# Delta-rule recurrence: the turned tile of updates, stored by value index instead of by lane, and read by the matmuls with a stride

## What is computed

```python
def step(S, inp):
    qt, kt, vt, at, bt = inp
    err = jnp.einsum('bhij,bhj->bhi', S, kt) - vt
    S = at[..., None] * S - bt[..., None, None] * (err[..., None] * kt[:, :, None, :])
    o = jnp.einsum('bhij,bhj->bhi', S, qt)
    return (S, o)
_, o = lax.scan(step, S0, xs)
```

## Time and profile before

| | |
|---|---|
| median of 3 runs | 3909.24 us (3908.29 to 3912.09) |
| span of the profiled execution | 3907.8 us |
| stretch with the recurrence | about 160 to 2345 us, 64 chunks of some 34 us |
| busy, whole span | PE 82%, DVE 76%, PEld 61%, POOL 56%, ACT 52% |

### The profile page before, as it was taken

The page is one execution under the profiler, slowest core; times in us unless marked ns, Lnnn a source line. Parts: engine busy times, 40 slices in busy tenths (PEclk is TensorE's granted clock), DMA queues, the critical chain, the costliest instruction groups (busy, mean ns, idle before and its releaser), DMA issues. The chain is left out here.

```text
span 3907.8 us, 126216 instructions
## 1 busy us (share of the span) xinstructions
PE 3194.9 (82%) x53441; PEld 2377.5 (61%) x53441; DVE 2965.5 (76%) x6600; ACT 2040.0 (52%) x4394; POOL 2182.6 (56%) x2735
## 2 busy tenths in 40 slices
PE   3678888887888888788888854759999899898989
PEld 2556666665666666666666644636666567656765
DVE  4488888888888888888888882058888788847884
ACT  2334444444444444444444423338887699728982
POOL 1367776767767677776767663431101188508860
PEclk7889999999999999999999975879999999999999
DMA  2111111111101111110111104100000012101111
GB/s 74 31 40 41 29 50 33 44 40 39 43 29 49 34 42 41 36 47 27 45 32 40 37 27 135 44 22 2 2 2 2 20 29 45 32 19 28 40 37 27
DMA packets 155957, 140.03 MB, mean 36 GB/s; under 512 B 64976, under 2 KB 108236, under 8 KB 155138
## 3 DMA queue, kind: packets, MB, share of 16 engines
q1 hardware_dynamic: 153090, 129.25, 12.0%
q0 software_dynamic: 2304, 2.71, 0.2%
HBM read 96.12 MB, written 16.82 MB: 29 GB/s over the span
## 5 line engine op out<-in xcount | busy, mean ns | idle before, releaser
L1235 DVE TENSOR_TENSOR a_tmp<-a_h,banks 128x128 f32<-128x128 f32 (+6 forms) x896 | 436.0, 487 | 29.9 <-DVE a_h L1212 0.2
L1241 DVE TENSOR_REDUCE a_h<-a_tmp 128x64 f32<-128x128 f32 (+6 forms) x896 | 432.2, 482 | 8.8
L940 POOL TENSOR_TENSOR a_st<-a_st,a_ab 128x512 f32<-128x512 f32 x256 | 322.1, 1280 | 0.0
L694 PE MATMUL banks<-a_wt,a_kt 32*64 32x64 f32 x8192 | 163.1, 258 | 145.8 <-DVE a_wt L1278 141.1
L552 PE MATMUL banks<-a_xseg,a_w_q 128*128 128x128 f32 x2048 | 247.0, 277 | 38.9 <-ACT a_kq L766 36.1
L2105 ACT ACTIVATE c_s<-c_s,c_low 128x384 f32<-128x384 f32 (+1 forms) x512 | 266.3, 579 | 19.1 <-DVE c_low L2049 13.7
L694 PEld LDWEIGHTS banks<-a_wt,a_kt 32*64 32x64 f32 x8192 | 153.6, 166 | 198.2 <-DVE a_wt L1278 169.8
L552 PEld LDWEIGHTS banks<-a_xseg,a_w_q 128*128 128x128 f32 x2048 | 234.3, 191 | 48.3 <-ACT a_kq L766 41.7
L2049 DVE CUSTOM_DVE_ANT_0 c_s<-banks,c_band 128x384 f32<-128x384 f32 (+1 forms) x512 | 245.5, 517 | 23.6 <-PE banks L1974 23.6
L552 PE MATMUL banks<-a_xseg,a_w_k 128*128 128x128 f32 x2048 | 241.5, 277 | 21.4 <-DMA a_xseg<-xn 18.4
L2150 POOL TENSOR_TENSOR c_qm<-c_qT,c_heads 128x512 f32<-128x512 f32 x32 | 33.3, 1040 | 396.3 <-PE banks L1974 395.9
(11 more groups left out here) (318 smaller groups left out, 8888.8 us busy)
## 6 DMA issues: line engine op xcount, KB each, us to landing
a_ab<-decays SPq DMA_DIRECT2D x512, 128.0 KB, 3.0
d_Vs<-d_V SPq DMA_DIRECT2D x128, 128.0 KB, 2.3
sent<-k_nothing SPq DMA_DIRECT2D x40, 64.5 KB, 2.3
b_xe<-sent SPq DMA_DIRECT2D x8, 322.5 KB, 3.4
a_xseg<-xn SPq DMA_DIRECT2D x32, 70.0 KB, 2.5
a_xrow<-in_L_attn_x SPq DMA_DIRECT2D x128, 16.0 KB, 1.8
x<-a_xrow SPq DMA_DIRECT2D x128, 16.0 KB, 1.6
back<-k_nothing SPq DMA_DIRECT2D x32, 64.0 KB, 1.6
```

Of the source, the lines that this page charges most:

```text
L694: t = e.matmul(self.ubank(bi)[par * DK:(par + 1) * DK, ct * DK:(ct + 1) * DK], self.Kt[rows, k0:k0 + DK], self.Wt[rows, x:x + 2, :].rearra ...
L940: e.tensor_tensor(sv, sv, self.ab[:, 8 * n:8 * n + 8, :], ALU.mult).then_inc(*self.s_decay.at((g, n)))
L1235: e.tensor_tensor(prod, both, gram, ALU.mult).then_inc(*step.at((g, t, "product")))
L1241: e.tensor_reduce(self.results(ch, t), prod, AX.X, ALU.add).then_inc(*step.at((g, t, "w")))
```

## The change

`self.Wt`, [128, 32, 32], was indexed (lane, i) and is now indexed (i, lane). Both DVE transposes write it in the order of their result blocks, so that the output is one run of 1024 adjoining floats, where before consecutive floats of a block went 32 floats apart. The moving operands of both products, 32 `i` of two lanes, were 64 adjoining floats, and are now 64 floats of which consecutive ones lie 32 floats (128 bytes) apart. The values, the order of the columns in PSUM, the number and the order of instructions on every engine, and all waits are the same.

```diff
@@ pe_cross
                     t = e.matmul(xb[rows, at:at + DK], self.Gx[rows, :, :, 8 * par + ct].rearrange("p z t -> p (z t)"),
-                                 self.Wt[rows, x:x + 2, :].rearrange("p h i -> p (h i)"), start=True, stop=True)
+                                 self.Wt[rows, :, x:x + 2].rearrange("p i h -> p h i"), start=True, stop=True)
@@ pe_U
                         t = e.matmul(self.ubank(bi)[par * DK:(par + 1) * DK, ct * DK:(ct + 1) * DK], self.Kt[rows, k0:k0 + DK],
-                                     self.Wt[rows, x:x + 2, :].rearrange("p h i -> p (h i)"), start=(pair > 0),
+                                     self.Wt[rows, :, x:x + 2].rearrange("p i h -> p h i"), start=(pair > 0),
                                      stop=(pair > 0 or ct == NCT - 1))
@@ dve_cross
-        e.transpose(self.Wt[:].rearrange("p x i -> p i x"), self.W[ch]).then_inc(*self.s_wm.at(g))
+        e.transpose(self.Wt[:], self.W[ch]).then_inc(*self.s_wm.at(g))
@@ dve_state
-        e.transpose(self.Wt[:].rearrange("p x i -> p i x"), Wc).then_inc(*self.s_wt.at(g))
+        e.transpose(self.Wt[:], Wc).then_inc(*self.s_wt.at(g))
```

## The result

Before 3910.34 us, after 3981.03 us (medians of 4 runs each): a ratio of 1.0178, 95% interval 1.0165 to 1.019. The kernel became 1.8% slower; the forecast was 2.9%, 4022 us. The profiled execution has a span of 3978.6 us, 70.8 more than before. From L1253 in chunk 0 to L1292 in chunk 63 it takes 2245.1 us where it took 2180.0, so 65 us lie in the recurrence. The other 6 us are about what the runs of the changed kernel scatter by (3974 to 3986).

A forecast was written before the change was run, and what follows sets the result against it. The recurrence, about 2180 of 3907.8 us, was taken as a DVE transpose, PE product, DVE loop. Losses of 98.6 + 49.6 + 19.8 = 168 us less 55 gained, net 113, gave 4022 us; own range 4004 to 4038.

The forecast's parts named there:

- The transposes: DVE's L1253 and L1278: from 1.995 and 1.981 to 1.24 us, saving 0.745 us 128 times, 55 of 95 us reaching the end.
- The price of the stride on the moving operand: Both products: 0.84 ns more a column, a group of four from 58 to 112 ns, 1.7 us on a function at full clock.
- no price: Rival: PE's moving stream does not care about the stride in either product, only savings remain; 3859 us, chance 0.11.
- half price: Rival: the stride costs the products' moving stream 0.42 ns a column; 3928 us, case up to 4004, chance 0.06.
- load and stream in turn: Rival: in `pe_cross` strided loads and stream no longer overlap, another 1.7 us 58 times; 4120 us, chance 0.05.
- shared read: Rival: `pe_U`'s two column strips take turns fetching from the same partitions, 7 us a `pe_U`; 4233 us, chance 0.07.
- the first rival: PE's moving stream in both products does not care about the stride, only 50 us of savings remain; 3859 us, chance 0.11.
- the list of savings: Shorter transposes without a product price: 15.0 (even `pe_cross`) + 23.8 (odd `pe_U`) + 22 x 0.5 (odd `pe_cross`), 50 us.
- `pe_cross`, even: Even chunks: product 1.7 us longer, less PE's present wait for the transpose, 0.47 us each, 15.0 us over 32 chunks.
- `pe_cross`, odd: Odd chunks: product 1.7 us longer; the shorter transpose saves 0.745 us in 22 of them, 16.4 us.
- `pe_U`, even: Even chunks: product from 1.99 to 3.7 us, 1.6 us each reaching the path, 49.6 us; no saving from the transpose.
- `pe_U`, odd: Odd chunks: product from 3.06 to 3.7 us, 19.8 us lost; the transpose saves 0.745 us each, 23.8 us.

The follow-up runs named there:

- `e7_write_step`: Changed kernel with the tile stretched: L1253 writes floats 12 bytes apart, L1278 8, products read 384 and 256 bytes apart; 3994.47 us in one run.
- `e4_pairs`: Against the kernel before: two neighbouring lanes side by side, transposes write runs of two floats, products read floats 8 bytes apart; 3856.2 us, ratio 0.9871.
- `e1_cross_only`: Against the kernel before: new layout for transpose L1253 and `pe_cross` only, L1278 and `pe_U` as before; 3975.12 us, ratio 1.0172.
- `e2_u_only`: Against the kernel before: new layout for transpose L1278 and `pe_U` only, L1253 and `pe_cross` as before; 3918.44 us, ratio 1.0021.
- `e3_u_odd`: Against the kernel before: new layout for L1278 and `pe_U` in odd chunks only; 3892.45 us, ratio 0.9964.

## Why the prediction was right, and where its sum was not

**The transposes** were priced right: 1.24 us forecast, 1.245 measured. The stride of the writes was their whole excess (`e7_write_step`).

By the time alone the full price is not confirmed: 3981 us lies in the span that the prediction left to the case of half the price (3928 to 4004). It is the durations that decide for the full price.

**The price of the stride on the moving operand**, taken from PE's loads, held: forecast 112 ns a group, measured 110 to 114 in most groups of both products; `pe_cross` was forecast at 3.7 us in all chunks, half clock or not, and takes 3.77. The rivals "no price", "half price", "load and stream in turn" and "shared read" all fall with these numbers. In `e4_pairs`, where the price is zero, the first rival's time came out: 3859 us forecast, 3856 measured, which checks the total of the list of savings. The rule that the prediction cites from the Trainium skill, "VectorE: DVE Perf Modes", section on mode 1x, falls as the prediction had it, since the transposes did get shorter. Two readings in this step were loose. The prediction took the loads with a step of 2 floats for ones without a price, which no row of before could show; `e4_pairs` shows it for the moving operand (58 ns a group). And the transposes' 1.99 us are 1.94 ns for each of 1024 elements, within the 1.6 to 1.8 named there only if a fixed part is taken off; nothing in the sum rests on it.

**`pe_cross`, even**, was forecast at 1.7 - 0.47 = 1.23 us a chunk; it is 1.20.

**`pe_cross`, odd**: the start was forecast 16.4 / 32 = 0.51 us earlier, and is 0.92 earlier, so the chunk lost 0.79 instead of 1.19 us. In `e1_cross_only` it lost 1.14, so this term was sized right for `pe_cross` by itself, and the difference came with the other half of the change. PE was late in eight of the 32 odd chunks before (by 2.9 us and more in seven), in seven after. In `e2_u_only`, where nothing at `pe_cross` changed, the start is 0.37 us earlier too (2.51 for 2.88), in `e3_u_odd` 0.24. The profile puts these late starts down to stalls of PE that nothing it shows releases ("issue"). I had taken them as fixed.

**`pe_U`, even**, is the term with the largest error, 1.6 us forecast and 0.85 measured. Two parts of it failed. The product grew by 1.40, not 1.7: where its first half (batches 0 and 1) meets the second, on other row strips, seven groups of chunk 38 follow each other in 44 to 70 ns instead of 112, so fewer than 32 full groups count. And `pe_P` did not hand on the delay of L1292: the second half of it waits for L1292 now (0.37 us in chunk 38), but before there was an "issue" stall of 0.80 us about there, which has gone. All "issue" idle time before L650, its loads included, fell from 86.1 to 18.7 us. The lower bound that I had beside it, 1.3, used the later start of `pe_P` with a `pe_U` of 3.7 us; with 3.39 it gives 0.99. `pe_P` started 0.87 later, and 0.85 is what came (1.03 in `e2_u_only`). I chose the wrong end.

**The stalls that went away.** In chunk 38 before, L650 was interrupted after 86 of its 128 matmuls; its second row has the 0.80 us:

```profile
1490.73 0.85 PE L650 MATMUL banks<-a_st,a_kq 64*32 64x64 f32 x42 [0.80 <-issue]
```

The traces point to the supply of instructions. The view of DMA queues of before, 200 to 2300 us, has this line (packets, MB):

```profile
q8 instruction: 299, 4.90, 1.0%
```

In that stretch PE has 76,355 matmuls and loads, 255 for each of these packets. Between 160 and 2346 us PE has 55 "issue" waits of over 0.4 us ahead of a matmul, 51.8 us together, and each of them ends 1.2 to 1.6 us after one of these packets has landed, though packets land some 7 us apart on the mean. In all ten traces it is 1.18 to 1.65 us. After the change 20 such waits are left, 24.8 us together. Where the even `pe_U` takes 2.0 us, in the five runs of that kind, `pe_P` behind it was stopped in 24 to 27 of 32 chunks (17.1 us in before); where it takes 3.4 or 3.5, in at most two. So a longer `pe_U` hides stalls that before stood open behind it, and this is what the prediction left out. No run changed the supply itself, so that it is the cause is read from these times and not tested.

**`pe_U`, odd**, was forecast at 0.62 - 0.745 = -0.12 us a chunk and is 0.16 - 0.71 = -0.56. The mean length is 3.44 us, not 3.7, for the same overlap, and half of what it grew was hidden by the turns of L1165 and L1191 on DVE before L1202, whose wait for PE I had not taken into that term.

**Together**: a pair was forecast to lose some 3.9 us and lost 2.31. The misses, 0.40, 0.75 and 0.43 us, make 1.6 us, in 29 pairs 46 us, 5 more than the 41 us between 4022 and 3981. All three lie on one side: the prediction had the durations right and let too much of them reach the end. The step that failed is the `pe_U` side of the path, 46 us in the sum and 9.5 measured.

## What to carry to other kernels

When a transpose moves a stride from its output to the reader of it, price both sides before choosing; here the write cost 0.745 us for 1024 floats a partition and the read 1.4 to 1.7 us in a product of 128 matmuls that ran side by side on four strips. Look for a layout that is fine for both: two floats in a row were enough for the writer and for the reader. Where TensorE ran at half clock, the stride of a float32 moving operand was nearly free. And price the waits behind a product that gets longer: some of its length may fall into stalls that stood there before.

## What the runs showed of the hardware

- The unit is 16 bytes, and what matters is whether two floats of it are used in a row. Step in bytes and time, DVE's write of 1024 floats: 4 and 8, 1.245 us; 12, 1.617; 128 to 384, 1.97 to 2.0; runs of 2 or 4 floats, 1.245. PE's moving read in `pe_cross` at full clock: 4, 2.07 us; 8, 2.09; 12, 3.07; 16, 3.94; 128, 3.77; 384, 3.78. That 16 bytes are a little slower than 128 was not expected, and no run says why.
- The Trainium skill, "SBUF — State Buffer", section on the DMA port swizzle, has the 16-byte line and a need for two hits on it. By that rule 8 bytes are free and 16 are not; these runs agree, and they give the size: 1.9 times the time for a float32 stream into TensorE at full clock (110 for 58 ns), 1.6 times for a DVE transpose (1.99 for 1.245 us).
- The price comes per stream and not per partition: in `pe_U` two streams read the same 32 partitions with the stride, and four still ran side by side at 110 to 114 ns.
